# Four pieces of the second unit's row maxima ahead of the first scores by key, in the first attention of an eight-part transformer kernel

## The reference, cut to what matters

```
B, S, D = 2, 1024, 128;  H, hd = 16, 8
qkv = layernorm(x) @ w_attn + b_attn          # split in q, k, v of 16 heads of 8
scores = einsum('bhqd,bhkd->bhqk', q, k) * hd ** -0.5
scores += mask      # key after query: -log(key - query + 1); key before query: -inf
attn = softmax(scores)                        # needs the maximum over the keys of each query
x = x + (einsum('bhqk,bhkd->bhqd', attn, v) reshaped) @ w_proj + b_proj
```

## Time and profile before

| | us |
|---|---|
| median of 3 runs | 1071.64 (1069.49 to 1075.83) |
| the profiled execution, its own time | 1072.73 |
| its span in the profile | 1070.9 |
| PE busy | 902.0 (84%) |
| DVE busy | 635.9 (59%) |
| POOL busy | 520.4 (49%) |
| ACT busy | 462.1 (43%) |
| mean granted clock of TensorE | 0.891 |

### The profile page before, as it was taken

The page is one execution under the profiler, slowest core; times in us unless marked ns, Lnnn a source line. Parts: engine busy times, 40 slices in busy tenths (PEclk is TensorE's granted clock), DMA queues, the critical chain, the costliest instruction groups (busy, mean ns, idle before and its releaser), DMA issues. The chain is left out here.

```text
span 1070.9 us, 18102 instructions
## 1 busy us (share of the span) xinstructions
PE 902.0 (84%) x6388; PEld 613.3 (57%) x6388; DVE 635.9 (59%) x1776; ACT 462.1 (43%) x1111; POOL 520.4 (49%) x500
## 2 busy tenths in 40 slices
PE   4768999999999988757998999995999995499992
PEld 2212333333334367644666889994885765489982
DVE  5776778676774545767776657773005565543333
ACT  2323666565565654335112757764533221032220
POOL 3445888878977932552322535555100001266651
PEclk9657999899999999778899799996999996599997
DMA  5800110110100000010000000302000000377764
GB/s 182 246 9 1 32 32 2 31 31 2 30 2 2 2 16 8 16 41 0 2 2 1 21 12 21 137 1 79 1 1 1 1 21 20 95 216 219 215 201 135
DMA packets 38751, 55.78 MB, mean 52 GB/s; under 512 B 7066, under 2 KB 26146, under 8 KB 38534
## 3 DMA queue, kind: packets, MB, share of 16 engines
q1 hardware_dynamic: 36166, 49.51, 15.5%
q0 software_dynamic: 2496, 5.12, 1.7%
HBM read 43.47 MB, written 10.94 MB: 51 GB/s over the span
## 5 line engine op out<-in xcount | busy, mean ns | idle before, releaser
L506 POOL TENSOR_TENSOR arena<-arena 128x1024 f32<-128x1024 f32 (+3 forms) x100 | 195.8, 1992 | 42.6 <-ACT arena L698 42.5
L698 ACT ACTIVATE arena<-ps 128x512 f32<-128x512 f32 (+3 forms) x320 | 137.8, 489 | 93.8 <-PE ps L602 63.6
L780 DVE CUSTOM_DVE_ANT_0 ps<-ps,arena 128x512 f32<-128x512 f32 (+3 forms) x256 | 148.7, 640 | 49.0 <-PE ps L571 48.1
L571 PE MATMUL ps<-arena 48*128 48x512 bf16 (+3 forms) x384 | 103.3, 368 | 25.3 <-DVE arena L780 16.0
L156 POOL TENSOR_SCALAR vareps<-meanvar 128x4 f32<-128x4 f32 x32 | 8.1, 252 | 183.7 <-DVE meanvar L103 182.8
L594 PE MATMUL ps<-arena 51*128 51x512 bf16 (+3 forms) x384 | 76.0, 350 | 5.8 <-DMA arena<-arena 5.2
L571 PEld LDWEIGHTS ps<-arena 48*128 48x128 bf16 x384 | 28.2, 95 | 92.0 <-DVE arena L780 55.1
L2261 PE MATMUL ps<-arena 128*128 128x128 f32 x624 | 78.8, 281 | 0.0
L2261 PEld LDWEIGHTS ps<-arena 128*128 128x128 f32 x624 | 75.3, 197 | 0.0
L776 DVE TENSOR_REDUCE arena<-ps 128x1 f32<-128x512 f32 (+3 forms) x128 | 55.8, 484 | 20.9 <-PE ps L571 20.3
L623 PE MATMUL ps<-arena 128*9 128x512 f32 (+3 forms) x640 | 66.7, 493 | 0.0
(11 more groups left out here) (349 smaller groups left out, 2074.3 us busy)
## 6 DMA issues: line engine op xcount, KB each, us to landing
arena<-in_L_ffn_w SPq DMA_DIRECT2D x39, 512.0 KB, 3.8
arena<-scratch SPq DMA_DIRECT2D x32, 192.0 KB, 4.0
arena<-in_L_ffn_w SPq DMA_DIRECT2D x16, 256.0 KB, 3.5
scratch<-arena SPq DMA_DIRECT2D x12, 256.0 KB, 2.9
arena<-expert_rows SPq DMA_DIRECT2D x8, 256.0 KB, 4.6
scratch<-arena SPq DMA_DIRECT2D x4, 384.0 KB, 2.8
scratch<-arena SPq DMA_DIRECT2D x12, 128.0 KB, 2.9
x<-in_x SPq DMA_DIRECT2D x4, 256.0 KB, 4.3
```

Of the source, the lines that this page charges most:

```text
L506: nc.gpsimd.tensor_tensor(e, e, weight[:, at:at + k].unsqueeze(1).broadcast_to([P, 2, k]), ALU.mult).then_inc(weighed, 1)
L571: nc.tensor.matmul(m.ps[:, (2 * k + e) % MAX_BANKS, 0:wd], qs[rows, u % BUFS, pair, i * P:(i + 1) * P], ks[rows, u % BUFS, pair, first:fir ...
L698: nc.scalar.activation(probs(g)[:, 2 * p + e, 0:wd], m.ps[:, BANK[h, e], 0:wd], ACT.Exp, scale=SCALE).then_inc(exps, 1)
L780: nc.vector.tensor_tensor_reduce(out=scores, in0=scores, in1=before[:, 0:wd], scale=-1.0, scalar=negrest[:, h, i:i + 1] if i < TPC else 3e ...
```

## The change

`pieces_at()` leaves out the first four pieces of the second unit (far 0 and near 0, both pairs), and `schedule()` puts them behind the first unit's split, turn and copy and in front of h0. The other 20 pieces are spread over the same window h0 to h13 by the same rule.

```
+    FIRST_OF = {1: 4}
...
             cost = [2 * piece_width(n) + 150 for n in range(NP)]
+            cost = cost[FIRST_OF[u]:] if u in FIRST_OF else cost
...
-                while n < NP and (spent + cost[n] / 2) * sum(span) <= gone * sum(cost):
-                    at.setdefault(h, []).append((u, n))
+                while n < len(cost) and (spent + cost[n] / 2) * sum(span) <= gone * sum(cost):
+                    at.setdefault(h, []).append((u, n + NP - len(cost)))
...
         yield from ((what, 0, 0) for what in ("split", "turn_max", "take_max"))
+        yield from (("max", 1, n) for n in range(FIRST_OF[1]))
```

More of the change, by code:

```diff
@@ L338, in pieces_at @@
                 gone += t
-                while n < NP and (spent + cost[n] / 2) * sum(span) <= gone * sum(cost):
-                    at.setdefault(h, []).append((u, n))
+                while n < len(cost) and (spent + cost[n] / 2) * sum(span) <= gone * sum(cost):
+                    at.setdefault(h, []).append((u, n + NP - len(cost)))
                     spent += cost[n]
                     n += 1
-            assert n == NP
+            assert n == len(cost)
         return at
```

## The result

The changed kernel took 1057.96 us (median of 5 runs, 1056.19 to 1062.03), before 1071.64 us: a ratio of 0.9867, 95% interval 0.9825 to 0.991. It is 13.7 us faster where about 5 were forecast (1067.0, range 1062 to 1072). Measured once more on another chip, the ratio was 0.9868 (0.9844 to 0.9892).

The account below looks back on a forecast made before the run. DVE, broken twice by PE, was taken as the path: 5.16 us of its work moved into 7.34 us idle, taken as 5.0. 1072.73 - 5.0 = 1067.7, or 1066.6 at the median; forecast 1067.0, range 1062 to 1072.

Parts of the forecast that it names:

- The hole: Before the second unit's first reduction: DVE idle falls from 7.34 to about 1.6 us; h0 stays at 72.4.
- The window: Second unit, h0 to h14: lead of 0.6 us at h4, 3.3 at the first product, about 5 at h14.
- The waits of DVE behind h4 and h8: DVE waiting for PE after these two halves with log: near 2.5 and 3.3 us.
- The clock's rise: TensorE's full clock at about 91 us instead of about 94.3, at the first product with the values and h8.
- Given back: Rival: PE is the path in the window or next units absorb the gain; 1.6 us, 1070; 0.22 with "doesn't do it".
- the clock stays low: Rival: from the first product the clock stays 1.2 GHz till the turn at 109; 1.9 us slower, 1074.6; chance 0.08.
- the very early rise: Rival: clock rises about 10 us earlier, around h4's log matmuls; 8.5 us gain, 1064; chance 0.10.
- Behind the window ... I count the gain once and carry it to the end.: From h14 on, lists are the same; the difference stays at 5 us to the end but for low-clock stretches.
- fall differently in each execution: Low-clock stretches like that at 200 us vary between executions; 2 us added on both sides of 1064.5 to 1069.5.

Follow-up runs that it names:

- the repeated profiles: Both kernels measured again unaltered: changed kernel 1056.9 us (0.9868), kernel before 1071.14 us (1.0).
- two, six and eight pieces: Changed kernel with that many pieces moved ahead instead of four: two 1069.14 us (0.9952; profiled twice), six 1061.77 us (0.9867), eight 1068.06 us (0.9964).
- dense: Units 3 to 8 with near 2 matmuls twice, far 3 four times: kernel before 1070.29 us (0.993), changed kernel 1065.91 us (0.9887 of before).
- delayed: Transposes of the second unit's maxima done four times over: kernel before 1074.36 us (0.9975), changed kernel 1071.84 us (0.9926 of before).

## Why the prediction was wrong

- *The hole.* Right. DVE's idle time was 1.65 us (1.6 forecast), h0 kept its place, and PE did not wait for the load.
- *The window.* Right in its steps and 0.9 us too small in its sum: 0.8, 3.1, 3.1, 4.5, 4.8 and 5.9 us of lead, where 0.6, 3.3, 3.3, 4.2, - and 5.0 were forecast. The waits of DVE behind h4 and h8 were 2.46 and 2.92 us (2.5 and 3.3). Most of the missing part lies behind h9, at full clock: from h9 to h14 it gained 1.4 us, not 0.8. The other pairs put it at 5.3 us (the repeated profiles, 37.61 and 32.27), 5.5 and 5.45. That the path is DVE's is shown by two, six and eight pieces: the gain grows with the DVE work in the hole, until the hole is full.
- *The clock's rise.* Right: 89.0 us, 90.4 on the scale of the profile of before, for 91 forecast, with the first product and h8. "Given back" and "the clock stays low" did not happen in this kernel, nor the very early rise. That the clock rose with this burst is not sure to repeat, as the first profile with two pieces shows.
- *"Behind the window ... I count the gain once and carry it to the end."* This step failed. The lists there are the same and so are the times, as long as the clock is full. But the clock isn't: before lost 8.3 us (11.0 in its second profile, less the same unit 8) to falls that the changed kernel doesn't have, for it arrives at other moments. I had seen the fall at 200 to 210 us and used it only as a doubt about the window. I also read it wrongly, as a clock that drops where PE looks busy: the 9.94 of 10 us lie behind the fall, at half clock, and in the 6 us ahead of it PE was busy 4.52. The range took the falls as chance that is alike on both sides, and added 2 us. The Trainium skill, "TensorE: Matmul & The Clock Gate", Part 1, says that the activity monitor runs free of the kernel, so that one kernel meets it differently from run to run; the prediction's "fall differently in each execution" assumes the same. For the later units these runs agree with it only in part. Units 2 and 3 of before did differ between two executions, but the falls of units 4 to 8 repeated, the changed kernel twice had that of unit 8 alone, and the two kernels' times on one chip do not overlap. Counting the falls would have given the right question: the full-clock lengths of the units (19.75, 19.48, 19.88, ...) against the actual ones say that 8.3 us were there to be won, and a change that shifts these units by one or two microseconds can win them or lose them. The range had to reach down by that.
- *What of the 13.7 us is the new order's own?* 5.3 to 5.9 us by the windows, and 4.4 (dense) and 2.5 to 5.3 us (delayed) by the totals of pairs with like falls. The other 8 us are real for this kernel and repeat, but a delay of 1.5 us takes 6.2 us away (0.9868 to 0.9926), its own 1.5 included, and 0.9 us of delay in the old order wins 5.8 us without the change. Luck has the larger share of the 13.7 us. Why the clock falls at one moment and not at another stays open.

## What to carry to other kernels

A hole in which the next stage's work can stand is worth the work of the engine that bounds the stretch behind it, and no more than the hole holds; fill it, and stop. When lists behind a change are the same, compare the lengths of repeated units at full clock first: if they agree and the totals don't, look at the granted clock. And before crediting a reordering with more than its own sum, run a pure delay in both versions: a gain that a delay destroys or makes is not the order's.

## What the runs showed of the hardware

- A fall of TensorE's clock between h4 and h8 lengthened that stretch by 1.4 to 1.5 us (clock 0.92 over it) or 3.5 to 3.9 us (0.78), in all kernels here.
- Whether it comes depends on when the place is reached to within tenths of a microsecond: units 2 and 3 fell in one profile of before and not in the other, with 26.9 and 26.5 us from the rise to unit 2. Unit 2 of the dense kernel of the old order, again at 26.9 us, fell too.
- The same six microseconds of work (PE busy 4.52 us in both) were followed by a fall in one kernel and by none in the other.
- Matmuls of 48 rows that kept PE busy 9.32 of 10 us, many of them repeats, left the clock at 0.50; products with the values or log matmuls, which use 128 rows, stood ahead of each rise in the window, but the log matmuls of h4 and, in one profile of two moved pieces, the first product with those of h8 brought none. Whether it is the rows is not tried.
